# Layer one's q, k and v of a two-layer vision tower: 64-feature tails as pairs of row halves, biases and positions added outside TensorE

## The reference

```python
h = tok_ref(x, W)                                  # 768 -> 192 per patch
qkv = h @ w_attn + b_attn                          # layer one
scores = q @ k.T * scale + (q * scale) @ rel.T     # rel: a row of rel_emb per key place, row 0 zero
h = layernorm(h + softmax(causal(scores)) @ v @ w_proj + b_proj)
probs = softmax(h @ Wg.T + bg); combine = its two largest
hw = (h @ A + ba) * combine
qkv = h @ Wqkv.T + bqkv + 2 * (hw @ Bm + combine @ bb)   # layer two
h = layernorm(h + softmax(q @ k.T * 0.25) @ v @ Wproj.T + bproj)
```

## The kernel before, in words

| slots | work |
|---|---|
| 7, 15, 25, 33, 41, 49 | E O1 R |
| 8, 16, 24, 28, 32, 36, 42, 50, 58 | Q2 T1 and O1 or O2 (or both) |
| 18, 26, 34, 44, 52 | Q2 T1 |
| 6, 10 | Q2 T1 R |
| 9, 11, 17, 19, 27, 35, 37, 43, 45, 51 | E Q1 R, most with O1 |
| 14, 40, 48, 56 | T1 and O2 only |
| 13, 21, 31, 39, 47 | Q1 O1 |
| 22, 30 | E O2 (22 also T1) |
| 5, 59 | T1 R, without Q2 (5 also Q1 O1) |

## Time and profile before

### The profile page before, as it was taken

How to read it: one execution, slowest core, us unless ns; L and a number is a source line. 1 busy time by engine, 2 the same in 40 slices (tenths; PEclk the granted TensorE clock), 3 DMA queues, 4 the chain that set the end, 5 groups by cost and what they waited for, 6 DMA issues and landing times.

```text
span 444.7 us, 13552 instructions
## 1 busy us (share of the span) xinstructions
PE 398.6 (90%) x5270; PEld 348.5 (78%) x5270; DVE 295.0 (66%) x783; ACT 231.7 (52%) x727; POOL 116.6 (26%) x237
## 2 busy tenths in 40 slices
PE   5874997999989999999999999989998999887974
PEld 4763886878878898889888899778886988776853
DVE  7051566857677676876687767696578758777572
ACT  1341455465565656555665555646655565544442
POOL 1110112230233213432242222333223223313122
PEclk9995999999999999999999999999999999996875
DMA  8452221210212111220221212111101110111010
GB/s 282 131 159 63 50 80 18 51 38 15 48 28 62 50 48 28 64 54 11 50 64 25 57 45 58 28 19 30 18 19 19 30 18 19 17 23 22 14 32 23
DMA packets 49353, 21.23 MB, mean 48 GB/s; under 512 B 41278, under 2 KB 45601, under 8 KB 49226
## 3 DMA queue, kind: packets, MB, share of 16 engines
q1 hardware_dynamic: 48714, 19.64, 18.1%
q10 hardware_dynamic: 576, 0.73, 0.5%
HBM read 13.13 MB, written 2.41 MB: 35 GB/s over the span
## 4 chain that ended last, share of the span: by engine, by line
PE 73%; ACT 9%; DVE 8%; issue 5%; DMA 3%; SPq 1%; POOLq 0%; POOL 0%; ACTq 0%; DVEq 0%
PE ps L414 11%; PE ps L484 10%; PE ps L497 8%; PE ps L472 7%; PE ps L519 5%; PE ps L508 5%; PE ps L449 4%; PE ps L453 4%; PE ps L451 4%; PE ps L436 3%; PE ps L438 3%; PE ps L520 3%; DVE mx L763 2%; PE ps L540 2%; ACT q L646 2%
## 5 line engine op out<-in xcount | busy, mean ns | idle before, releaser
L763 DVE TENSOR_REDUCE mx<-ps 113x12 f32<-113x588 f32 x64 | 49.2, 769 | 75.4 <-PE ps L472 74.8
L378 POOL TENSOR_SCALAR kbd<-k,const 64x294 f32<-64x294 f32 x128 | 69.1, 549 | 98.1 <-ACT q L646 88.0
L667 ACT COPY pt<-ps 113x339 f32<-113x339 f32 x128 | 50.7, 445 | 52.1 <-PE ps L497 51.7
L385 POOL TENSOR_SCALAR shift<-mv,rstd 128x1 f32<-128x1 f32 (+1 forms) x50 | 13.2, 264 | 216.4 <-ACT rstd L702 216.4
L414 PE MATMUL ps<-tokw,xs 128*128 128x192 f32 (+1 forms) x300 | 57.1, 342 | 9.1 <-DVE res L791 4.8
L775 DVE TENSOR_REDUCE psum<-probs 113x12 f32<-113x588 f32 x64 | 48.4, 756 | 23.7 <-ACT probs L653 22.9
L414 PEld LDWEIGHTS ps<-tokw,xs 128*128 128x128 f32 (+1 forms) x300 | 50.7, 197 | 11.4 <-DVE res L791 6.4
L497 PE MATMUL ps<-const,probs 113*113 113x113 f32 x384 | 52.1, 274 | 3.4 <-DVE probs L784 2.6
L784 DVE TENSOR_TENSOR probs<-probs,rsum 113x588 f32<-113x588 f32 x64 | 51.4, 802 | 2.2
L497 PEld LDWEIGHTS ps<-const,probs 113*113 113x113 f32 x384 | 47.2, 186 | 6.6 <-issue 5.1
L770 DVE TENSOR_TENSOR probs<-ps,mx 113x588 f32<-113x588 f32 x64 | 49.4, 772 | 2.2
(11 more groups left out here) (79 smaller groups left out, 704.2 us busy)
## 6 DMA issues: line engine op xcount, KB each, us to landing
xs<-in_x SPq DMA_DIRECT2D x24, 384.0 KB, 3.7
vbd<-vrow SPq DMA_DIRECT2D x160, 18.4 KB
out<-o SPq DMA_DIRECT2D x24, 96.0 KB, 1.7
tail<-in_pos SPq DMA_DIRECT2D x1, 656.0 KB, 16.2
tokw<-in_tokw ACTq DMA_DIRECT2D x3, 192.0 KB, 3.4
w<-in_w SPq DMA_DIRECT2D x1, 472.5 KB, 10.0
xs<-in_x SPq DMA_DIRECT2D x3, 128.0 KB, 3.2
p<-in_p SPq DMA_DIRECT2D x2, 145.5 KB
```

The lines of the kernel that those rows point to most:

```text
L378: last = nc.gpsimd.tensor_scalar(L.kbd[t % 2][:, e], L.k[:, :, at:at + T], kmask[:, e:e + 1], 1.0, ALU.mult, ALU.mult)
L667: nc.scalar.copy(pt[n % 2][:, 3 * half:3 * half + 3, :].rearrange("p g i -> p (g i)"), ps[0:PP, 2 + half, 0:3 * PP]).then_inc(pt_ready[hal ...
L763: nc.vector.tensor_reduce(mx[:].rearrange("p (b h) -> p b h", b=2), score_view, AX.X, ALU.max).then_inc(mx_ready, 1)
```

## The change

Layer one's second operand becomes `ht0[:, b, 1, :]`: the 64 tail features twice, in rows 0 to 63 and again in rows 64 to 127. The weights of the chunks 0 and 1 stand in the lower row half, those of chunk 2 and of v in the upper. `project_qkv1` issues the four full products first and then the tails, alternating between the halves; a chunk's lower half and the one beside it lie in different banks. Banks 4 and 5 now hold q, k and v. Biases and positions are a table `add1`: VectorE adds it as it takes q and k out of PSUM in one instruction (`take_qk1`, at the end of its slot, instead of ScalarE's two copies), and GpSimd adds the bias to v in place (`bias_values`). q and k lie in one tensor `qk1` of 128 rows; the 0.25 is now multiplied in as `kbd` is made.

```diff
-            def project_qk1(b, free):
-                k, lo = tokens(b), first_token(b)
-                if free:
-                    pe.wait_ge(*free)
+            def project_qkv1(b, *free):
+                k = tokens(b)
+                for emptied in free:
+                    if emptied:
+                        pe.wait_ge(*emptied)
+
+                features, rest = ht0[:, b % HB, 0, :], ht0[:, b % HB, 1, :]
+
+                def chunk(m):
+                    return ps[:, 4:6, :].rearrange("p b n -> p (b n)")[:, 256 + m * NB:256 + m * NB + k]
+
+                values = ps[:, 5, NB:NB + E]
+
                 for m in range(3):
-                    nc.tensor.matmul(ps[:, 4, m * NB:m * NB + k], w1a[:, m * 128:(m + 1) * 128],
-                                     ht0[:, b % HB, 0:k], start=True, stop=False)
-                    last = nc.tensor.matmul(ps[:, 4, m * NB:m * NB + k], w1b[0:TAIL, m * 128:(m + 1) * 128],
-                                            tail[0:TAIL, lo:lo + k], start=False, stop=True)
-                last.then_inc(L1.qk_done, 1)
+                    nc.tensor.matmul(chunk(m), w1a[:, m * NB:(m + 1) * NB], features[:, 0:k], start=(m != 1), stop=False)
+                nc.tensor.matmul(values, features, w1a[:, V0:V0 + E], start=False, stop=False)
+
+                nc.tensor.matmul(chunk(0), w1b[0:64, 0:NB], rest[0:64][:, 0:k], start=False, stop=False)
+                nc.tensor.matmul(chunk(2), w1b[64:128, 0:NB], rest[64:128][:, 0:k], start=False, stop=False)
+                nc.tensor.matmul(chunk(1), w1b[0:64, NB:2 * NB], rest[0:64][:, 0:k], start=False, stop=True
+                                 ).then_inc(L1.qk_done, 1)
+                nc.tensor.matmul(values, rest[64:128], w1b[64:128, NB:NB + E], start=False, stop=True
+                                 ).then_inc(L1.v_done, 1)
                 return L1.qk_ready, b + 1
 
...
             def take_ht(b):
...
-                nc.scalar.copy(ht0[:, b % HB, 0:k], ps[:, 6, 0:k])
-                nc.scalar.copy(tail[0:64, lo:lo + k], ps[0:64, 6, 128:128 + k]).then_inc(ht_ready, 1)
+                nc.scalar.copy(ht0[:, b % HB, 0, 0:k], ps[:, 5, 0:k])
+                for p0 in (0, 64):
+                    last = nc.scalar.copy(ht0[p0:p0 + 64, b % HB, 1, 0:k], ps[0:64, 5, NB:NB + k])
+                last.then_inc(ht_ready, 1)
...
+            def take_qk1(b):
+
+                dve.wait_ge(L1.qk_done, b + 1)
+                dve.wait_ge(L1.v_rows, b + 1)
+                gone = last_tile(b) - RING // T
+                if gone >= 0:
+                    dve.wait_ge(scores_done, SLOT1[gone] + 1)
+                src = ps[:, 4:6, :].rearrange("p b n -> p (b n)")[:, 256:256 + 3 * NB].rearrange("p (m n) -> p m n", m=3)
+                place = first_token(b) % S
+                for slot, at, k in pieces(b):
+                    last = nc.vector.tensor_tensor(qk1[:, :, slot:slot + k], src[:, :, at:at + k],
+                                                   qk_add[:, :, place + at:place + at + k], ALU.add)
+                last.then_inc(L1.qk_ready, 1)
+
...
+            def bias_values(b):
+                nonlocal upper
+                k = tokens(b)
+                if b == 0:
+                    pool.wait_ge(add1_loaded, 16)
+                pool.wait_ge(*moved_k)
+                pool.wait_ge(L1.v_rows, b + 1)
+                nc.gpsimd.tensor_tensor(L1.vrow[b % VR][0:k], L1.vrow[b % VR][0:k], v_add[0:k], ALU.add
+                                        ).then_inc(v1_ready, 1)
+                upper = v1_ready, b + 1
+
```

```diff
                 for b in turns(n):
...
-                    bank6 = project_v(L1, b, values1(b), bank6)
-                    bank4 = project_qk1(b, bank4)
+                    bank4 = bank5 = project_qkv1(b, bank4, bank5)
+                for b in turns1(n):
+                    bank6 = transpose_h1(b, bank6)
                 for b in embeds(n):
-                    bank5 = embed(b, bank5)
+                    bank7 = embed(b, bank7)
...
                 for b in routers(n):
-                    transpose_hw(b)
+                    bank6 = transpose_hw(b, bank6)
                 for b in turns1(n):
                     if b == 0:
                         pe.wait_ge(lora_loaded, 16)
-                    route(b)
+                    bank7 = route(b, bank7)
```

```diff
                 if before:
                     take_pt(n - 1)
-                for b in turns1(n):
-                    take_h1(b)
...
                 for b in turns(n):
-                    take_v(L1, b, SLOT1)
-                    take_qk(L1, b, SLOT1)
+                    take_v(L1, b, NB, SLOT1)
+                for b in turns1(n):
+                    take_h1(b)
```

More of the change, by code:

```diff
@@ L194, in build @@
         w1a = sb("w1a", [128, 3 * E])
-        w1b = sb("w1b", [128, 3 * E])
+        w1b = sb("w1b", [128, V0 - 256 + E])
+        add1 = sb("add1", [128, 3 * AW + 3 + E])
+        qk_add = add1[:, 0:3 * AW].rearrange("p (m n) -> p m n", m=3)
+        qk_bias = add1[:, 3 * AW:3 * AW + 3]
+        v_add = add1[:, 3 * AW + 3:3 * AW + 3 + E]
         p1 = sb("p1", [C + 1, 2, E])
@@ L291, in build @@
         w1b_loaded = sem("w1b_loaded")
-        pos_loaded = [sem(f"pos_loaded{u}") for u in range(2)]
+        add1_loaded = sem("add1_loaded")
+        add1_ready = sem("add1_ready")
+        v1_ready = sem("v1_ready")
         p1_loaded = sem("p1_loaded")
@@ L400, in _ @@
                 block_diagonal(n + 2)
+                for b in turns(n):
+                    bias_values(b)
         @block.tensor
@@ L832, in combine @@
                     comb[0:k, 1:1 + NE][:, :, None].to_broadcast([k, NE, R]), ALU.mult).then_inc(hw_ready, 1)
-            for n in range(SLOTS):
+            for n in range(FIRST, SLOTS):
                 layer, t = attention(n)
@@ L888 @@
     order += [2 * E + (4 * u + 2 * g + e) * 16 + d for e in range(2) for u in range(3) for d in range(16) for g in range(2)]
-    is_k = [part for m in range(3) for part in range(2) for _ in range(64)]
     order = _np.array(order)
-    k_cols = _np.flatnonzero(_np.array(is_k) == 1)
     wa = a['L0_attn_w_attn'][:, order]
     w1a = wa[0:128]
-    w1b = zeros(128, 3 * E)
-    w1b[0:64] = wa[128:E]
-    w1b[65:64 + S, k_cols] = _np.tile(a['L0_attn_rel_emb'][0:S - 1], (1, len(k_cols) // 16))
-    w1b[64 + S] = a['L0_attn_b_attn'][order]
-    pos = zeros(64, TOK)
-    pos[0:S] = _np.tile(_np.eye(S, dtype=_np.float32), (1, TOK // S))
-    pos[S] = 1.0
+    w1b = zeros(128, V0 - 256 + E)
+    w1b[0:64, 0:256] = wa[128:E, 0:256]
+    w1b[64:128] = wa[128:E, 256:]
+    add1 = zeros(128, 3 * AW + 3 + E)
+    add1[:, 3 * AW:3 * AW + 3] = a['L0_attn_b_attn'][order[0:V0]].reshape(3, 128).T
+    rel = zeros(S, 16)
+    rel[1:] = a['L0_attn_rel_emb'][0:S - 1]
+    places = rel[_np.arange(AW) % S].T
+    for m in range(3):
+        add1[64:128, m * AW:(m + 1) * AW] = _np.tile(places, (4, 1))
+    add1[:, 3 * AW + 3:] = a['L0_attn_b_attn'][order[V0:]]
     const = zeros(128, 266)
@@ L904 @@
     const[:, 128:256] = _np.tile(_np.eye(64, dtype=_np.float32), (2, 2))
-    for p in range(64):
+    for p in range(128):
         const[p, 256 + p // 16 % 2] = 1.0
@@ L927 @@
     arrays, args = {}, []
-    for name, laid in (('x', px), ('tokw', tokw), ('w1a', w1a), ('w1b', w1b), ('pos', pos), ('const', const),
+    for name, laid in (('x', px), ('tokw', tokw), ('w1a', w1a), ('w1b', w1b), ('add1', add1), ('const', const),
                        ('p1', p1), ('lora', lora), ('w2', w2), ('b2', b2), ('p2', p2)):
```

127 lines of the change are left out of this document (71 added, 56 removed).

## The result

The changed kernel takes 488.6 us (median; 481.8 to 495.0), against 448.2 for the kernel before: a ratio of 1.077, interval 1.063 to 1.092. It is slower, near the forecast of 490. The profiled execution, the longest of the four, took 495.0 us, with a span of 493.2. One kernel's own runs differ with the granted clock (those of the changed kernel have spans of 480.0 and 483.3 us at a mean clock of 0.92, and of 490.3 and 493.2 at 0.90 and 0.89), so the ratios leave out a kernel's runs that are over 1.5% above its fastest, while the medians are over all.

What follows compares the result with a forecast made beforehand. From about 40 us one queue of TensorE work was taken to bound the kernel. Terms summed to +26 us, 473 against the profiled 446.5; clock falls added 16, the median 1: 490 us, range 466 to 508.

Steps and rivals of the forecast that it cites:

- Part 1: Layer one's tails on TensorE run as pairs: 0.24 to 0.34 us saved a block, -6 us (0 to -9.7).
- Part 2: ScalarE's second 64-row feature copy before layer one's projections adds 0.16 us of TensorE wait a block, +3.6 us.
- Part 3: `take_h1` at the end of ScalarE's slot makes TensorE's `route` wait for `h1t`: +18.6 us together.
- Part 4: Patch product in bank 7 waits for VectorE's `hw`: +11.7 us in six slots, +2.7 us in ten.
- Part 5: Small waits: output projection for `hwt` +1.2 us; old waits taken away -2.5, -0.2 and -1.5 us.
- Part 6: VectorE's add (about 555 ns) and GpSimd's (0.5 to 0.8 us) hidden, apart from light slots counted in Part 3.
- Part 7: At the start, 550 KB less to load at 362 GB/s ahead of the first placed values: -1.4 us (0 to -2).
- Part 8: Behind the new waits the clock falls to half in four or five of six places, 10.24 us each: +16 us.
- The rival without clock falls: New waits on TensorE, no further clock falls: 473 to 476 us; chance with none, one or two falls 0.28.
- The rival *faster: On TensorE the pairs decide and the waits for `h1t` and `hw` are hidden: about 436 us, chance 0.04.
- No change within 2%: One of the two TensorE waits real, the other not, no clock fall: 455 to 458 us, chance 0.06.
- That the pairs don't pair: Layer one's tails do not run in pairs on TensorE: 7 us more than forecast, within the range; no separate chance.

Runs made afterwards that it cites:

- e5: e3 with the tail products over all 128 rows, the unused half of the weights zero, nothing paired: 446.1 us, 0.988 of the kernel before.
- e8: e3 without the last of the three feature copies, so some products lack their 64-feature part: 441.5 us, 0.976 of the kernel before.
- e1: The changed kernel with `take_h1` back ahead of the q and k copies on ScalarE: 460.6 us, 1.029 of the kernel before.
- e3: The changed kernel with `take_h1` moved back and the patch product in bank 6 again: 449.0 us, 0.993 of the kernel before.
- e6: e3 with the three loads of 97 rows each cut into 96 rows and one row: 437.3 us, 0.975 of the kernel before.
- e11: The kernel before with only its 97-row loads cut into 96 rows and one row: 438.0 us, 0.973 of the kernel before.
- e4: The changed kernel with unread matmuls ahead of the waiting `route` and patch product, all waits kept: 466.8 us, 1.041 of the kernel before.
- e10: e9 with the tails as full 128-row products, as in e5: 437.0 us, 0.972 of the kernel before.
- e7: e3 with a semaphore for the first feature copy, so 128-feature products start before the 64-row copies: 445.7 us, 0.996 of the kernel before.
- e9: e3 with the cut loads of e6 and the stepwise feature copies of e7: 439.0 us, 0.978 of the kernel before.

## Where the prediction was right and where it was wrong

The time, the direction and the two main steps were right; several sizes were not, and their errors offset one another. That the median lies within 2 us of the forecast is luck: the kernel's own runs lie 13 us apart.

*Part 1, pairs.* Put at 0.24 us a block (0.34 ahead of V x P), measured 0.15 and 0.25. They do run over each other, and each change of shape costs its 0.10: the first tail follows the last full product after 0.42 us (220.54 to 220.96) where in e5 it is 0.32. The missing 0.09 is in the first pair, whose second pass starts 0.22 us after the first (220.96, 221.18) and not 0.11 like that of the next (221.29, and 221.40 after it). With 4 us a kernel the term lay between the -6 taken and the -2.6 that followed from reading the Trainium skill's rule of a drain at a mode switch (TensorEngine Tiling (Array Packing), Key Properties) as the whole difference between length and pace.

*Part 2, the third copy.* Put at 0.16 us a block, measured 0.27: from the last transpose to the first projection 0.54 us, against 0.27 before, and 0.27 again in e8. The copies of 64 rows follow each other after 0.26 us, not after the 0.16 that lay between a copy of 128 and one of 64 rows. 22 blocks make 5.9 us instead of 3.6; with part 1 the change of layer one saves TensorE at best nothing: -0.15 + 0.27 = +0.12 us a block, or +0.02.

*Part 3, `take_h1`.* 18.6 us expected, 17.4 us of waits in 18 places measured, and e1 took them away. `route` was to come 1.22 us late in slot 24; in slot 28, which is like it and free of other shifts, it starts 7.19 us after the slot's start instead of 5.79, 1.4 late. In slot 24 itself it is 0.66 late (7.23 instead of 6.57): TensorE got through the slot's first part sooner than before, by more than the 0.22 us that were reckoned with. The light slots lose by a wait that the prediction doesn't have. `transpose_h1` now shares bank 6 with the output projection and waits for the residual add, 4.2 us in slots 14, 22, 40 and 48. TensorE in slot 14 of the kernel after:
```profile
127.60 0.42 PE L578 MATMUL ps<-const,h 128*96 128x128 f32 x2 [1.09 <-DVE res L854]
...
129.12 0.47 PE L588 MATMUL ps<-lora,h1t 96*128 96x136 f32 x2 [0.62 <-ACT h1t L726]
```
Slots 14, 40 and 48 are 1.2 to 1.6 us longer than before, and with `take_h1` moved back, in e1, still 0.7 us. Slot 56, which has no add of q and k in the slot before it, has no such wait: the delay by VectorE's add, priced at 0.5 us in part 3, is in it. No run takes this wait away; e3 and all versions built on it have it.

*Part 4, the patch product.* 11.7 + 2.7 us expected, 11.2 in six places measured; late by 1.85 where 1.95 was worked out. In slots with a projection ahead the 2.7 us don't show: in slots 27 and 35 the product starts 4.81 us after the slot's start instead of 4.69, and 0.12 is what parts 1 and 2 make of the block.

*Part 5.* Of the small waits the one of the output projection for `hwt` shows (1.7 us in 3 places on PE, 4.3 in 12 on PEld; 1.2 expected) and ScalarE's `yt` fell from 6.7 us in 16 places to 4.2 in 9, 2.5 instead of 1.5. No run tells these apart.

*Part 6.* The groups of the kernel after, by shape (busy us, mean ns, idle before):
```profile
L419 POOL TENSOR_TENSOR vrow<-vrow,add 128x192 f32<-128x192 f32 x24 | 14.2, 591 | 2.1
...
L832 DVE TENSOR_TENSOR qk<-ps,add 128x384 f32<-128x384 f32 x19 | 10.5, 551 | 9.9 <-ACT vrow L706 9.9
```
551 ns against 555 worked out, 591 between the bounds of 0.5 and 0.8 us, and nobody on TensorE waits for either. The add does delay VectorE's next maximum by 0.5 us in more slots than the light ones (22, 24 and 32 too); what that costs wasn't tried.

*Part 7, the start.* The step that failed by its mechanism. I took 550 KB at 362 GB/s, -1.4 us. The first V x P product came 4.1 us earlier (35.73 against 39.84), because SyncE's standstills are shorter: 4.0 and 5.5 us, where they were 4.3 and 8.3 in the kernel before, which has one more load between the two of 97 rows. So `w` is issued at 15.2 us, and 3.8 us later in the kernel before. What the start waited for were the issues behind the 97-row loads, as e6 and e11 show, and the prediction has no row of SyncE's queue. Whether the missing load or its bytes shortened the second standstill wasn't tried.

*Part 8, the clock.* The price was right and the number wrong. I took 3.5 us for a fall of 10.24 us, 0.34 us for each us, and e4 shows 0.36. I expected four or five falls of 10 us, and there were ten, most of them of 3.4 to 6.8 us, 54.6 us at half clock, and outside this stretch 14 us more than before. The kernel after has 68.6 us more at half clock than the kernel before in its profiled run, and some 37 more in its two shortest, which makes 13 to 24 us; the 16 expected lie between.

The sum without the clock was +26 and is some +24 by e4 at equal clock. With the measured terms of parts 1 to 4 and 7 it would be -4 + 5.9 + 17.4 + 11.2 - 4.1 with part 5's -3.0, some +23. So close an agreement is luck too, as part 5's term is the expected one and the light slots' wait is in none. The rival without clock falls was wrong by the trace and, as e4 shows, would have been 467, at the low end of the range. The rival *faster* is added up wrong: its terms give 432, not 436, which changes no chance. No change within 2% would have needed one of the two waits to be absent, and both were there. That the pairs don't pair was wrong; that they bring nothing was nearly right in the time all the same.

## What to carry to other kernels

Where an in-order queue is nearly full, ask of every moved statement what will wait behind it: a copy of 0.38 us moved behind two copies and a Ln and Exp, and a bank shared with a later reader, cost 40 us, and the edit they belonged to was worth nothing that could be measured. Before a gain or a loss of a few us is put down to an edit, compare the time that its runs spent at half clock (e5 and e10 looked faster than they were). A wait of one or two microseconds on a busy TensorE costs more than itself if the clock falls behind it; try matmuls that nobody reads in its place, and measure a change again when the clock is held, since a gain (e7, e9) can hide behind more falls. Look at the first microseconds of the issuing queue: one load that holds it up delays all behind it.
